# The order of the second attention's projections and transposes on TensorE

## The reference, cut to what matters

```python
q = (x @ w_q)            # 32 heads of 128, rotated (rope)
k = (x @ w_k)            # 8 key heads of 128, rotated, each shared by 4 query heads
v = (x @ w_v)            # 8 value heads
lk = ((x @ w_lq) @ w_lk) # 32 key heads of the latent attention, rotated
lv = (x @ w_lv)          # 32 value heads of the latent attention
attn = causal_softmax(q @ k.T / sqrt(128)) @ v
lat  = causal_softmax(q @ lk.T / sqrt(128)) @ lv
out  = attn @ w_o + lat @ w_lo
```

## Time and profile before

| What | Value |
|---|---|
| median of three runs | 2584.31 us |
| the profiled execution | 2582.9 us |
| its span in the trace | 2580.8 us |
| TensorE busy | 2364.9 us (92%) |
| VectorE busy | 1773.9 us (69%) |
| ScalarE busy | 1459.6 us (57%) |
| GpSimd busy | 1568.7 us (61%) |
| second attention, from first to last scores | 930 to 2313 us of the span |

### The profile page before, as it was taken

The page is one execution under the profiler, slowest core; times in us unless marked ns, Lnnn a source line. Parts: engine busy times, 40 slices in busy tenths (PEclk is TensorE's granted clock), DMA queues, the critical chain, the costliest instruction groups (busy, mean ns, idle before and its releaser), DMA issues. The chain is left out here.

```text
span 2580.8 us, 44531 instructions
## 1 busy us (share of the span) xinstructions
PE 2364.9 (92%) x14333; PEld 2053.6 (80%) x14333; DVE 1773.9 (69%) x3131; ACT 1459.6 (57%) x3978; POOL 1568.7 (61%) x1320
## 2 busy tenths in 40 slices
PE   8899999993899889999899999998999999987998
PEld 7788888882488778888788888887888888875886
DVE  3566656665923269888788888888888888972232
ACT  1466656661043346667666667666676666664432
POOL 2555555630044277887787878878778878751442
PEclk8899999996599989999999999999999999997999
DMA  2101010101000021110111111101101111003000
GB/s 96 31 23 41 23 41 18 33 1 41 0 1 1 29 64 35 47 55 17 57 45 36 47 42 43 44 29 52 54 24 55 37 42 48 23 5 139 1 17 17
DMA packets 41352, 93.75 MB, mean 36 GB/s; under 512 B 4836, under 2 KB 6760, under 8 KB 39808
## 3 DMA queue, kind: packets, MB, share of 16 engines
q1 hardware_dynamic: 41092, 90.55, 10.9%
HBM read 79.78 MB, written 10.75 MB: 35 GB/s over the span
## 5 line engine op out<-in xcount | busy, mean ns | idle before, releaser
L1095 POOL TENSOR_TENSOR a_nf_acc<-a_nf_acc,a_nf_term 128x512 f32<-128x512 f32 (+1 forms) x416 | 588.6, 1415 | 143.0 <-ACT a_nf_term L1189 72.6
L1575 POOL TENSOR_TENSOR f_w_lo<-WGU,f_w_hi 128x512 fp32r<-128x512 f32 x88 | 114.9, 1307 | 347.8 <-ACT f_w_hi L1591 347.6
L1149 ACT ACTIVATE a_probs<-bank,a_dip 128x128 f32<-128x128 f32 (+1 forms) x512 | 208.3, 419 | 199.5 <-DVE a_dip L1430 199.5
L1158 ACT ACTIVATE a_probs<-a_probs,a_share 128x128 f32<-128x128 f32 (+1 forms) x512 | 192.4, 464 | 61.5 <-DVE a_share L1436 61.5
L1076 POOL TENSOR_TENSOR a_qk_lo<-a_straight,a_qk_hi 128x512 fp32r<-128x512 f32 (+1 forms) x160 | 194.3, 1216 | 47.5 <-ACT a_qk_hi L1135 47.5
L63 PE MATMUL bank<-a_wo_hi,a_ot_hi 128*128 128x512 f32 x512 | 212.3, 415 | 0.0
L365 POOL TENSOR_TENSOR a_straight<-a_straight,a_crossed 128x512 f32<-128x512 f32 x64 | 82.4, 1288 | 212.9 <-DVE a_crossed L718 212.9
L1500 DVE TENSOR_SCALAR a_nf_term<-a_nf_unit 128x512 f32<-128x512 f32 (+1 forms) x288 | 203.6, 751 | 3.4 <-DVE a_nf_unit L1483 0.6
L1441 DVE TENSOR_TENSOR a_pt_lo<-bank,a_pt_hi 128x384 fp32r<-128x384 f32 x256 | 140.9, 550 | 93.8 <-ACT a_pt_hi L1166 93.2
L65 PE MATMUL bank<-a_wo_hi,a_ot_lo 128*128 128x512 f32 x512 | 201.3, 393 | 0.0
L64 PE MATMUL bank<-a_wo_lo,a_ot_hi 128*128 128x512 f32 x512 | 201.0, 392 | 0.0
(11 more groups left out here) (247 smaller groups left out, 8633.0 us busy)
## 6 DMA issues: line engine op xcount, KB each, us to landing
a_raw<-in_l_o SPq DMA_DIRECT2D x64, 256.0 KB, 2.6
a_raw<-in_l_vk SPq DMA_DIRECT2D x32, 384.0 KB, 3.1
a_raw<-in_l_ql SPq DMA_DIRECT2D x32, 320.0 KB, 2.9
a_raw<-in_l_ou SPq DMA_DIRECT2D x32, 288.0 KB, 2.8
n_codes<-coded_w SPq DMA_DIRECT2D x8, 1056.0 KB, 13.1
a_raw<-in_l_nr SPq DMA_DIRECT2D x16, 384.0 KB, 3.0
a_nf_raw<-in_w_nf SPq DMA_DIRECT2D x24, 256.0 KB, 2.6
coded_w<-a_nf_acc SPq DMA_DIRECT2D x24, 256.0 KB, 2.0
```

What stands on the lines that cost most here:

```text
L1095: pool.tensor_tensor(acc, left, nf_term[:, i % CODE_RING, 0:w], ALU.add).then_inc(nf_added, 1)
L1149: act.activation(probs[:, n % 2, col:col + keys], bank[:, at:at + keys], ACT.Exp, bias=dip[:, n % 2, i:i + 1], accum_out=total[:, n % 2, i ...
L1158: ins = act.activation(cell, cell, ACT.Copy, scale=share[:, n % 2, i:i + 1])
```

## The change

In the second attention's step, the loop that projects the further units is put ahead of `turn(n - 1, 1)`. Everything else, the other engines' orders included, stays.

```diff
                     if not (first and n < 3):
                         output(n - 3)
+                    for name in units[1:]:
+                        project(name)
                     if not (first and n < 1):
                         turn(n - 1, 1)
-                    for name in units[1:]:
-                        project(name)
```

## The result

The changed kernel takes 2637.19 us (median of four runs, 2636.03 to 2642.68) against 2586.02 us of the kernel before (four runs, 2582.13 to 2592.98): 1.0194 times as long, 95% interval 1.0175 to 1.0214, 51 us slower. Forecast were 2652 us, in a range of 2608 to 2673.

A forecast was written before the change was run, and what follows sets the result against it. The prediction took the chain of VectorE and ScalarE to set the pace in most steps. To 2582.9 us it added 64 us for delayed steps, net of group ends, and 5 us for the clock: 2652 us, range 2608 to 2673.

The forecast's parts named there:

- What bounds the stage: Second attention: the chain of VectorE and ScalarE sets the pace in most steps, though busy share points to TensorE.
- Steps with one further unit cost nothing: Steps 0, 2, 3, 4, 6, 7, 8, 15: the delay is hidden, 0, bounds 0 and +0.3 us a step.
- Steps with two pay: Steps 1, 5, 9, 10, 11, 14: second transposes wait behind A's rotation, +1.2 to +1.9 us each.
- The sum for step 1: Step 1 of a loop group: copy of A starts at about 1301.4 instead of 1300.20, +1.2 us.
- Sum of 8.7 us a group: Loop group: 1.2 + 1.2 + 1.5 + 1.9 + 1.2 + 1.7 us for steps 1, 5, 9, 10, 11, 14.
- Rival 2: Second attention: the wait only moves, VectorE hides the rest; 2583 us, give or take 10; chance 0.07.
- The clock: Step 5: the joined 2.7 us wait lowers TensorE's clock in three of eight groups, 5 us in all.
- rival 4: The clock falls in most groups, in steps 9 or 10 too; 2661 to 2674 us; chance 0.2.
- The ends of the groups: Step 15 wins 0.5 us in groups 1 to 5; entries to groups 1 and 7 win 0.4 us each.
- walk: The step-by-step pricing of the delays within a group, 8.7 us for a loop group.
- Rival 1: Second transposes, L1304: the freed waits stay free, some 40 us faster, 2543 us; chance 0.05.
- Rival 3: Only steps 10 and 14, partly 9 and 11, pay: some 4 us a group, 2615 us; chance 0.13.

The follow-up runs named there:

- the filled kernel: The changed kernel with ten extra 512-column products into the free scores bank ahead of K in step 5 of every group: 2607.65 us, 1.0085.

## Why the prediction was right, and which terms were off

- *What bounds the stage*: right. VectorE and ScalarE set the pace, and the busy share of TensorE misled. Shown by the kernel with only the first unit ahead: 34 us of TensorE's wait moved, time unchanged.
- *Steps with one further unit cost nothing*: right, 0.9989.
- *Steps with two pay, since the transposes come to stand behind the rotation*: right in sign, place and mechanism; these steps alone give 1.0207. With GpSimd's sums cut all six were sized within 0.05 us, in the full kernels steps 1, 10 and 14 within 0.2. The sum for step 1 should read 1301.5 and +1.3, and for group 0 nothing is measured where +0.7 was taken.
- *Sum of 8.7 us a group*: too large, 6.0 us where the clock held. The term that was mis-sized is the one set at zero, that the delayed work of VectorE keeps its length. L1415 of K and of step 12 shrank by 0.55, 0.88 and 1.16 us. Rival 2 named this and I gave it a chance only as a whole; it was a part of the forecast case.
- *The clock*: right that it falls at a wait of 2.7 us, too low in number: seven groups of eight, not three. Against the filled kernel, where it held everywhere, step 5 costs 8.7 us more in eight groups. With the 1.3 us of step 11 in group 7, a place that only rival 4 came near, the clock is worth 10 us, where 5 were forecast.
- *The ends of the groups*: 3.3 us were taken off, for step 15 and the two entries. From step 15 to step 1 of the next group the two traces have 1.3 us more in sum after the change, not less. The single heads scatter by up to 2 us between them, so that VectorE catches up there is not shown.
- *The sum.* From the first to the last peaks of the second attention the change costs 57.9 us in the traces: 10 of clock, 1.3 at the ends of the groups and 46.6 in steps 1 to 14, where 5, -3.3 and 67.4 were forecast. The two spans differ by 53.4 us only, because the changed kernel's trace reached the second attention 4.8 us sooner, in code that the change does not touch. The forecast missed by 15 us. Its largest error, 21 us of walk too much, was met by two of opposite sign, 5 us each, so that the miss wasn't larger is in part luck.
- *Rival 1*, faster by 40 us, is out by the runs with only the first unit ahead (1.0002) and with only the steps of one unit (0.9989). *Rival 3*, half of it, had its mechanism wrong: the lag of steps 1 and 5 isn't gone by step 9, and these steps pay.

## What to carry to other kernels

Before moving work ahead of a wait, list the waits of the moved work: what stood behind the old wait now stands behind those. Where two engines hand each other buffers in turn, ask which of them has idle time; a wait on the engine that is busy to 92% can be worth nothing, and the cheap test is to move it and see whether another wait grows by the same amount. In a chain priced from rows of an engine that shares with a neighbour, look at the spread of the same instruction: a row at twice its shortest time may shrink when it is moved.

## What the runs showed of the hardware

- Ten extra products ahead of a loop, 20 instructions in the trace, made a kernel 24 us faster (2637.19 to 2613.26 us). Some 21 of 27 us in the traces are one of two stops that went from the head of each of five loop passes. That the place of the loop's code does it is likely and not shown; in any case an experiment that adds instructions needs a control that adds them outside the place under test.
- After waits of 2.6 to 2.8 us the granted clock fell in six groups of seven in one kernel and in four of seven in another. Where it fell in the first of them, the step took 0.5 to 1.6 us longer than in the filled kernel. A wait of that length is a risk and not a fixed price. "TensorE: Matmul & The Clock Gate" of the Trainium skill (What's actually happening) says that the chip judges by a window that runs freely and isn't aligned with the kernel; that the same wait had both outcomes agrees with it.
- VectorE's sum of two SBUF operands, 128x512, took 0.69 to 1.86 us in one kernel; with GpSimd's sums cut its mean fell from 999 to 711 ns, and that of the 128x256 one from 1000 to 426.
